# Layer norms two and four scaled on ScalarE, and the router's logits issued quarter by quarter

## The reference

```python
x = x + attn0(layernorm(x))    # local window + chunked linear attention, gated mix
x = x + moe(layernorm(x))      # 8 experts, sigmoid router, top 4 of 2 groups, and a shared expert
x = x + delta(layernorm(x))    # gated delta rule, 16 heads of 8
x = x + mix(layernorm(x))      # token shift, r * (relu(k)^2 W_v)

def layernorm(x): return (x - mean(x)) / sqrt(var(x) + 1e-5)      # no gain, no shift
# the router in moe: scores = sigmoid(x @ gate_w.T), 8 numbers a token
```

## Time and profile before

| | |
|---|---|
| median of 3 runs | 919.32 us (918.39 to 922.0) |
| the profiled execution | 919.77 us, its span in the trace 918.0 us |
| busy in the span: PE, DVE, ACT, POOL | 69%, 70%, 42%, 31% |
| mean granted TensorE clock | 0.844 of full speed |
| second norm with its projection, to the last logit | 493.3 to 516.7 us |
| last norm, from its first update to the first product of the last stage | 883.8 to 901.2 us |

### The profile page before, as it was taken

The page is one execution under the profiler, slowest core; times in us unless marked ns, Lnnn a source line. Parts: engine busy times, 40 slices in busy tenths (PEclk is TensorE's granted clock), DMA queues, the critical chain, the costliest instruction groups (busy, mean ns, idle before and its releaser), DMA issues.

```text
span 918.0 us, 22815 instructions
## 1 busy us (share of the span) xinstructions
PE 636.6 (69%) x9634; PEld 452.8 (49%) x9634; DVE 640.3 (70%) x1232; ACT 381.0 (42%) x905; POOL 286.7 (31%) x276
## 2 busy tenths in 40 slices
PE   3899999899999999999997789894200000000686
PEld 1688887566666666666566555474000000000674
DVE  6367876376766676666746562467999999998767
ACT  2556666532333333332223221237655454444124
POOL 6456555100000000000020001202578788787310
PEclk9989999999999999999999599997655555555567
DMA  5100000000000000000000013000000000000001
GB/s 188 21 6 14 15 15 13 3 3 2 11 5 2 4 12 2 2 2 2 2 3 1 1 34 60 1 1 1 0 0 0 0 0 0 1 0 0 2 1 46
DMA packets 8069, 11.05 MB, mean 12 GB/s; under 512 B 1296, under 2 KB 5648, under 8 KB 7840
## 3 DMA queue, kind: packets, MB, share of 16 engines
q1 hardware_dynamic: 7968, 9.60, 4.0%
HBM read 6.41 MB, written 1.08 MB: 8 GB/s over the span
## 4 chain that ended last, share of the span: by engine, by line
PE 55%; DVE 22%; issue 13%; POOL 5%; ACT 3%; DMA 1%; SPq 0%; DVEq 0%; POOLq 0%; ACTq 0%
PE PS L587 9%; PE PS L562 7%; PE PS L460 5%; PE PS L356 4%; PE PS L344 4%; PE PS L330 4%; PE PS L717 3%; PE PS L579 2%; PE PS L467 2%; PE PS L730 2%; PE PS L294 2%; DVE arena L1267 2%; DVE arena L1275 2%; PE PS L731 2%; POOL arena L1154 1%
## 5 line engine op out<-in xcount | busy, mean ns | idle before, releaser
L643 DVE TENSOR_TENSOR arena<-PS,C 128x512 f32<-128x512 f32 x160 | 105.5, 686 | 97.0 <-PE PS L562 97.0
L934 PE MATMUL PS<-arena 64*64 64x8 f32 x112 | 8.4, 255 | 196.3 <-DVE arena L1319 192.3
L1051 ACT ACTIVATE arena<-arena 128x128 f32<-128x128 f32 x256 | 81.8, 390 | 94.3 <-DVE arena L1275 94.3
L934 PEld LDWEIGHTS PS<-arena 64*64 64x64 f32 x112 | 7.1, 212 | 199.0 <-DVE arena L1287 193.9
L587 PEld LDWEIGHTS PS<-arena 128*64 128x64 f32 x2560 | 83.6, 138 | 40.0 <-issue 38.1
L1549 POOL TENSOR_TENSOR arena<-arena 128x512 f32<-128x512 f32 x4 | 5.0, 1274 | 305.0 <-PE PS L587 305.0
L562 PE MATMUL PS<-arena 64*64 64x512 f32 x640 | 87.1, 614 | 3.4 <-ACT arena L516 2.0
L1137 POOL TENSOR_TENSOR arena<-arena 128x1024 f32<-128x1024 f32 x32 | 75.2, 2350 | 41.6 <-DVE arena L1275 41.6
L587 PE MATMUL PS<-arena 128*64 128x18 f32 x2560 | 87.2, 211 | 0.0
L418 POOL TENSOR_TENSOR arena<-arena 128x512 f32<-128x512 f32 x64 | 66.6, 1041 | 54.5 <-DVE arena L401 50.7
L491 ACT ACTIVATE arena<-PS 128x512 f32<-128x512 f32 (+1 forms) x48 | 23.5, 524 | 129.9 <-PE PS L462 71.8
(11 more groups left out here) (252 smaller groups left out, 1470.6 us busy)
## 6 DMA issues: line engine op xcount, KB each, us to landing
W<-wpack SPq DMA_DIRECT2D x1, 2532.5 KB, 10.9
arena<-arena SPq DMA_DIRECT2D x128, 16.0 KB
arena<-carry_in SPq DMA_DIRECT2D x4, 512.0 KB, 7.8
X<-x SPq DMA_DIRECT2D x4, 256.0 KB, 3.7
out<-X SPq DMA_DIRECT2D x4, 256.0 KB, 2.3
C<-cpack SPq DMA_DIRECT2D x1, 529.0 KB, 6.5
wk<-wkT SPq DMA_DIRECT2D x1, 64.0 KB, 10.9
wv<-wvT SPq DMA_DIRECT2D x1, 64.0 KB, 11.4
```

The lines of the kernel that those rows point to most:

```text
L643: e.tensor_tensor(AT[n % 4].rearrange("p (h t) -> p h t", h=8), PS[:, n % 2, :].rearrange("p (h t) -> p h t", h=8), tri.to_broadcast([P, 8 ...
L1051: e.activation(Ra[:, cols], Rs[(t - 1) % 4][:, cols], ACT.Copy, scale=alp[:, t, h:h + 1]).then_inc(l_Ra, 1)
```

## The change

For norms 1 and 3 VectorE no longer makes the four scales. It makes one small product for each quarter, `shft = -mean * rstd` (128 x 4), and ScalarE makes the four tiles as `Identity(X * rstd + shft)` in a new `ln_scale_act`, right behind `ln_root`. In norm 1 VectorE's part of quarter q - 1 moves behind the moments of quarter q. The logits of quarter q - 2 are issued behind `ln_turn` of q - 1, into bank 1, which was free there; the first products no longer wait for the sigmoid, the second do.

```diff
@@ ln_scale
             e.wait_ge(ln_rstd, 4 * k + q + 1)
+            if k in (1, 3):
+                e.scalar_tensor_tensor(shft[:, 4 * q:4 * q + 4], mv[:, 4 * q:4 * q + 4, 0], -1.0, sd[:, 2, 4 * q:4 * q + 4],
+                                       ALU.mult, ALU.mult).then_inc(ln_shft, 1)
+                return
...
+        def ln_scale_act(e, k, q):
+
+            e.wait_ge(ln_shft, 4 * (k // 2) + q + 1)
+            for j in range(4 * q, 4 * q + 4):
+                e.activation(H[:, j, :], X[:, j, :], ACT.Identity, scale=sd[:, 2, j:j + 1], bias=shft[:, j:j + 1]).then_inc(ln_h, 1)
@@ moe_pe
-            for j in range(NT):
-                e.wait_ge(ln_hT, 4 + j // 4 + 1)
-                m = e.matmul(PS[:, 0, j * NE:(j + 1) * NE], htile(j), w("gateT"), start=True, stop=True,
+        def logits(e, q):
+            e.wait_ge(ln_hT, 4 + q + 1)
+            for j in range(4 * q, 4 * q + 4):
+                m = e.matmul(PS[:, 1, j * NE:(j + 1) * NE], htile(j), w("gateT"), start=True, stop=True,
                              skip_group_check=True)
             m.then_inc(f_lg, 1)
+
+        def moe_pe(e):
+            logits(e, NQ - 1)
...
-                if n == 0:
+                if n == 1:
                     e.wait_ge(f_sc, 1)
@@ end of the delta rule, ScalarE
                 ln_root(e, 3, q)
+                ln_scale_act(e, 3, q)
@@ second norm, ScalarE
                     ln_root(e, 1, q - 1)
+                    ln_scale_act(e, 1, q - 1)
@@ second norm, TensorE
                     ln_turn(e, 1, q - 1)
+                if q >= 2:
+                    logits(e, q - 2)
             ln_turn(e, 1, NQ - 1)
+            logits(e, NQ - 2)
             moe_pe(e)
@@ second norm, VectorE
                 ln_moments(e, 1, q)
-                ln_scale(e, 1, q)
+                if q >= 1:
+                    ln_scale(e, 1, q - 1)
+            ln_scale(e, 1, NQ - 1)
```

More of the change, by code:

```diff
@@ L77, in program @@
         sd = sb("sd", [P, 3, NT])
+        shft = sb("shft", [P, NT])
         arena = sb("arena", [P, AREN])
@@ L206, in program @@
         x_upd = sem("x_upd")
+        ln_shft = sem("ln_shft")
         xbo = sem("xbo")
@@ L698, in bc @@
             return ap.to_broadcast(shape)
-        def moe_pe(e):
-            for j in range(NT):
-                e.wait_ge(ln_hT, 4 + j // 4 + 1)
-                m = e.matmul(PS[:, 0, j * NE:(j + 1) * NE], htile(j), w("gateT"), start=True, stop=True,
+        def logits(e, q):
+            e.wait_ge(ln_hT, 4 + q + 1)
+            for j in range(4 * q, 4 * q + 4):
+                m = e.matmul(PS[:, 1, j * NE:(j + 1) * NE], htile(j), w("gateT"), start=True, stop=True,
                              skip_group_check=True)
             m.then_inc(f_lg, 1)
+        def moe_pe(e):
+            logits(e, NQ - 1)
             def down(tb):
@@ L860, in moe_act @@
         def moe_act(e):
-            e.wait_ge(f_lg, 1)
-            e.activation(rt_s.rearrange("p j e -> p (j e)"), PS[:, 0, 0:NT * NE], ACT.Sigmoid).then_inc(f_sc, 1)
+            e.wait_ge(f_lg, NQ)
+            e.activation(rt_s.rearrange("p j e -> p (j e)"), PS[:, 1, 0:NT * NE], ACT.Sigmoid).then_inc(f_sc, 1)
             for n in range(5 * NQ):
```

## The result

The changed kernel takes 933.42 us (median of 4 runs, 928.53 to 937.46) where the kernel before, run beside it, takes 920.66: ratio 1.0139 (95% interval 1.0104 to 1.0174), 12.8 us slower. The forecast was 10.2 us slower; the median lies 0.4 us above the range's top. The profiled execution is the fastest of the four, 928.53 us.

The account below looks back on a forecast made before the run. VectorE's list was taken to set the pace in both norms; after the change, closed rings of waits. Second norm +6.2 and last norm +4.0 give +10.2 us on the median of 919.32: 929.5, range 924 to 933.

Parts of the forecast that it names:

- the ring: Second norm: update, `shft`, scale, mixT, project and next update wait for each other in a closed loop; +6.2 us.
- The ring of the last norm: Last norm: `shft`, scale, store, own, shift, update and next `shft` wait in a closed loop; +4.0 us.
- VectorE's load decides: Rival, both norms: ScalarE's list is not in the ring, VectorE's round falls to 2.5 us; -10.8 us, 908.5; chance 0.05.
- round 1 of the second norm: Second norm, from update 1 to update 2 at 504.0: 6.7 us where it was 3.59.
- round 2: Second norm, update 2 at 504.0 to update 3 at 512.15, with four logits and project(3) at half clock.
- The recorded sum: Whole kernel: second norm 6.2 plus last norm 4.0, +10.2 us.
- The price of a scale: ScalarE, both norms: one scale with two pointers 479 ns, four overlapping 1.64 us; VectorE paid 1.11.
- the nearest row's 1.28: Both norms: four scales cost 1.28 us if the second column is free; whole sum 2.5 us smaller.
- The smaller-loss rival: Both norms: rings close, but scales cost 1.28 or logits run at full clock; 924 to 927; chance 0.12.
- The clock gives it back: Rival, second norm and experts' head: logits between turns keep TensorE at full clock; +4.4 us, 923.7; chance 0.08.
- No table load: Whole kernel: a rival that the change costs a table load was excluded; the list has 18 before and now.

Follow-up runs that it names:

- the shift in place: Changed kernel, with VectorE's reciprocal and `shft` of the second norm put back behind the moments of their own quarter; ratio 1.0025, second norm 19.60 us.
- the second trace: Trace of the changed kernel run once more with no edit; ratio 1.0148, 931.78 us.
- the ring kept warm: Changed kernel, with 16 idle matmuls on TensorE between each project and the turn behind it in the second norm; ratio 1.0100.
- the last norm alone, once more: Second run of the kernel before with only norm 3's scale on ScalarE; ratio 1.0040 (12 runs).
- the last norm alone: Kernel before with only norm 3's scale moved to ScalarE, first time; ratio 1.0094 (6 runs).

## Why the prediction was right or wrong

**Mechanism: right, but for one link.** Scales that wait for `shft`, `shft` behind the next quarter's moments, and updates that wait for project are in the timelines one behind the other, and the shift in place, which moves two small instructions on VectorE and nothing else, takes 10 us off the same stretch. The prediction named mixT as the link from scale to project. In the changed kernel no engine waits for mixT (L1632); the chain that ended last goes from the scales over the turn, and turn64 or the logits, to project, and the recorded times went that way too. So the condition on which the prediction let the ring hang, mixT behind the scale, did not bind there; whether mixT ahead of the scale would change anything was not tried. The ring of the last norm is shown by the order of own and scale, for half of its loss. The rival by which VectorE's load decides fell with its busy share: 33%, and the time rose.

**The step that failed: round 1 of the second norm was priced at full clock, and project in round 2 too low.** The recorded sum took turn64(3) at 1.08 and project(2) at 1.16, full clock. From start to next start they took 1.90 and 1.73: TensorE had waited 2.98 us for the scales, the clock fell during the turn behind that wait, and it was 0.50 from 501.0 to 504.0. Update 2 came 8.13 us behind update 1, and 8.51 in the second trace, forecast 6.7. Round 2 was forecast at half clock, and the logits took 1.73 there, forecast 1.71; but project(3) took 2.05, forecast 1.73, and the round 8.40, forecast 8.15. That 1.73 comes from a row in which the granted clock was 0.50 to 494.0 and 1.00 from 494.6; wholly at half clock project took 2.05 to 2.08 in these traces. The prediction took half clock because TensorE "now waits more", and took it one round too late. That the longer wait is what lowers the clock is not shown: in the ring kept warm TensorE had waited only 1.23 us at this place, behind idle matmuls, and the clock fell all the same. The second norm lost 7.8 and 8.2 us in the two traces, forecast 6.2; in the first, round 1 is 1.4 of the 1.6 us between.

**The last norm: right.** 21.04 against 17.07 to 17.43, so 3.6 to 4.0; forecast 4.0.

**The sum and the range.** By stretches 11.8 us, by the ratios 12.8 (9.6 to 16.0) and 13.6 (10.7 to 16.5); forecast 10.2, which the first interval holds and the second does not. So it is the stretches that show the shortfall, and it alone does not carry the time over the range's top of 933: 919.32 + 11.8 is 931.1. Of the 3.9 us between 929.5 and 933.42, 1.6 are the second norm's, 1.3 are the kernel before, whose median was 920.66 beside the result and 919.32 ahead of it, and 1.0 is not placed, in runs that go from 928.5 to 937.7. The range's top had 0.6 for project(2) at half clock, 2.7 for scatter, and nothing for turn64(3).

**The price of a scale: right.** 481 ns each, 1.65 us for four, where the nearest row's 1.28 was the rival. The prediction's estimate from the Trainium skill, "ScalarE: Activation LUTs", section "What ACT_TABLE_LOAD costs", 479 ns and 1.64 us, agrees with this trace. **The smaller-loss rival** fell with the 1.65 us and with the half clock at the logits. **The clock gives it back** fell as well: the granted clock is 0.50 from 507.8 to 528.2. Behind that the second spread did come 4.38 us behind the first, before 5.61; but the last norm alone, once more, with the code of before in this place, has 4.32, so this is not the change's. **No table load** was added: the trace has 18, as before.

## What to carry to other kernels

Before work is moved from a full engine to an idle one, follow one item round all engines in their written order: if the moved instruction waits for something that stands behind the next item's step, and that step stands behind the moved instruction, on its new engine or behind what uses its result on a third one, engines that overlapped now take turns, and busy shares won't tell. The cure here was order, not price: the same instructions with the small product in its own quarter were 10 us faster. And where a wait on TensorE grows, work out the matmuls behind it at half clock too, from the first round on: here that was 1.4 us in one round. Take the price at half clock from a row that was at half clock throughout.

## What the runs showed of the hardware that was not expected

In the kernel before, the logits kept TensorE busy for 6.65 us without a gap, and the granted clock stayed at 0.50 through them and behind them, to 528.5. With idle matmuls in the waits ahead of the logits and behind them it was 1.00 for 37 us.

Runs of one kernel spread over 6 to 10 us (before: 915.3 to 925.3 in 23 runs), and the traces place part of that in code that is the same: the middle took 363.3 to 367.0 us. The time goes with the mean granted clock of the run: of those 23, the six fastest (915.3 to 917.9) had 0.847 to 0.850 and the six slowest (922.0 to 925.3) 0.834 to 0.841. One place where it shows is the experts' head: with the same code, the second spread came 5.6 us behind the first in the traces of before and of the last norm alone, and 4.3 in that of the last norm alone, once more. What sets the clock from run to run was not tried.
